# Sparse cross-attention's preparation joined into its main block, its last two tiles weighed by VectorE and its last sums in one group, and the alignment's two edge moves swapped

## The reference, cut to what matters

```python
R = D[i, j] + min(R[i-1, j], R[i, j-1], R[i-1, j-1])     # cost table, 64 x 1601 per batch
# then backtracking through R from the end gives which context rows belong to each row of x
```

```python
Q, K, V = split_heads(x @ Wq.T + bq), split_heads(ctx @ Wk.T + bk), split_heads(ctx @ Wv.T + bv)
scores = Q @ K.T / sqrt(8)
topk_scores, topk_indices = top_k(scores, 32)
context = softmax(topk_scores) @ V[topk_indices]
x = x + (merge_heads(context) @ Wo.T + bo)
```

## Time and profile before

| what | value |
|---|---|
| median of 3 executions | 4256.11 us (4254.29 to 4256.95) |
| the profiled execution: its time, its span | 4252.25 us, 4250.5 us |
| busy over the span: TensorE, VectorE, ScalarE, GpSimd | 82%, 77%, 65%, 34% |
| alignment's scans | about 139 to 312 us |
| sparse cross-attention with its preparation | about 2625 to 4038 us |

### The profile page before, as it was taken

One profiled execution on the slowest core, in us unless ns is written; L12 is line 12 of the kernel. 1 busy time (PEld: TensorE's weight loads), 2 busy tenths in 40 slices (PEclk: granted clock), 3 DMA queues, 4 the chain that ended last, 5 costly groups with the idle time before them and its releaser, 6 DMA issues. The chain is left out here.

```text
span 4250.5 us, 71372 instructions
## 1 busy us (share of the span) xinstructions
PE 3506.3 (82%) x25855; PEld 2847.3 (67%) x25855; DVE 3271.4 (77%) x5582; ACT 2742.5 (65%) x4270; POOL 1437.4 (34%) x1185
## 2 busy tenths in 40 slices
PE   6435748999999879999999986788888888888787
PEld 3334437999999657799999963466666666666676
DVE  4684877777777652787787755899999999999744
ACT  3112626666666443666666642799999999999832
POOL 0000502111111100211122010577777777777610
PEclk9555869999999889999999988899999999999998
DMA  8744001111111020111111000100000000100000
GB/s 275 117 47 124 4 28 45 40 40 32 32 35 30 14 77 14 47 32 32 40 34 38 17 16 10 38 18 30 16 17 32 16 17 16 32 16 9 1 24 19
DMA packets 186346, 161.34 MB, mean 38 GB/s; under 512 B 7996, under 2 KB 174092, under 8 KB 185996
## 3 DMA queue, kind: packets, MB, share of 16 engines
q1 hardware_dynamic: 182604, 142.83, 12.9%
q10 hardware_dynamic: 3392, 13.93, 0.9%
HBM read 127.36 MB, written 20.20 MB: 35 GB/s over the span
## 5 line engine op out<-in xcount | busy, mean ns | idle before, releaser
L559 PEld LDWEIGHTS psU<-ctxN,ST 128*128 128x128 f32 x6656 | 853.7, 191 | 98.4 <-issue 39.6
L559 PE MATMUL psU<-ctxN,ST 128*128 128x129 f32 x6656 | 868.1, 275 | 20.6 <-issue 20.6
L645 ACT ACTIVATE ST<-ST 128x512 f32<-128x512 f32 (+1 forms) x832 | 513.3, 625 | 167.0 <-DVE ST L747 163.1
L1188 DVE MAX8 top<-pairs 128x8 f32<-128x1602 f32 (+1 forms) x384 | 587.6, 1535 | 0.0
L1143 POOL TENSOR_TENSOR P<-P,EX 128x1601 f32<-128x1601 f32 x128 | 460.4, 3597 | 305.7 <-ACT P L1046 305.7
L747 DVE TENSOR_TENSOR ST<-ST,psB 128x512 f32<-128x512 f32 (+1 forms) x832 | 555.8, 677 | 3.4 <-PE psB L578 3.4
L733 DVE TENSOR_TENSOR psA<-psA,ST 128x512 f32<-128x512 f32 x640 | 446.2, 697 | 137.4 <-ACT ST L637 69.5
L947 PE MATMUL psU<-ctxN,PT 128*128 128x129 f32 (+1 forms) x3328 | 454.3, 291 | 3.3 <-ACT PT L1054 3.3
L947 PEld LDWEIGHTS psU<-ctxN,PT 128*128 128x128 f32 (+1 forms) x3328 | 427.0, 206 | 3.8 <-ACT PT L1054 3.8
L547 PE MATMUL psS<-statL,ctxH 128*128 128x512 f32 x832 | 393.3, 473 | 5.6 <-ACT ST L637 2.7
L925 PE MATMUL psS<-KT,stat 128*128 128x512 f32 (+1 forms) x1024 | 379.4, 513 | 17.4 <-DVE maxes L1166 16.4
(11 more groups left out here) (509 smaller groups left out, 6686.0 us busy)
## 6 DMA issues: line engine op xcount, KB each, us to landing
ctxN<-in_ctx SPq DMA_DIRECT2D x48, 768.0 KB
ahead_ctxT<-ctxT_scratch SPq DMA_DIRECT2D x32, 800.5 KB, 4.3
ctxT_scratch<-trn ACTq DMA_DIRECT2D x16, 800.5 KB
ctxT<-ctxT_scratch SPq DMA_DIRECT2D x16, 800.5 KB, 6.1
nat<-in_ctx SPq DMA_DIRECT2D x16, 768.0 KB
dist_scratch<-dd SPq DMA_DIRECT2D x8, 800.5 KB
skewed<-in_ctx SPq DMA_DIRECT2D x8, 768.0 KB
ctx_late<-in_ctx SPq DMA_DIRECT2D x8, 768.0 KB
```

Source lines behind the costliest of these rows:

```text
L559: last = pe.matmul(psU[:, q, 0:D + 1], ST[0:n, i % SLOTS, q * 128:q * 128 + 128], ctxN[0:n, j, k, 0:D + 1], start=(k == 0 and q % 2 == 0), ...
L645: act.activation(ST[0:n, i % SLOTS, :], ST[0:n, i % SLOTS, :], ACT.Exp).then_inc(exp_done, 1)
L1188: dve.max(top_t[:, 8 * n:8 * n + 8], own).then_inc(listed_early if n < 2 else listed_late, 1)
```

## The change

Four edits, all to the order and the place of work; what is computed stays the same.

1. The alignment: in TensorE's and in ScalarE's list the drift's edge is now moved ahead of the cost's in every iteration.
2. The preparation of the sparse cross-attention: the six small blocks are gone. The `layernorm` block now also loads the first batch's transposed context (one 800 KB transfer, fourth of nine) and fills the constants. All the rest stands in the lists of the large block: three transposes, the queries in two halves, the first keys and scores, and, between the first scores, the joined weights in four products (their copies are now ScalarE's), the bias row, and the addition of the bias to x (GpSimd, in iteration 2).
3. The last two tiles (126 and 127): ScalarE makes the mask in one step, and VectorE's one instruction `weigh` takes the minimum with the count and multiplies with the exponentials; in iteration 128 ScalarE exponentiates tile 127 and marks tile 126 before its other work.
4. The last output product is one group: 12 heads between the transposes and the values of tile 127, 4 heads at the end, one addition.

```diff
+        wide_Wo = P[:].rearrange("p j k -> p (j k)")[:, 0:H * D]
+        BY_VECTOR = T - 2
+        layernorm(c, [(W[:, 0, :], d["L3_xattn_Wq"]), (W[:, 1, :], d["L3_xattn_Wk"]),
+                      (W[:, 2, :], d["L3_xattn_Wo"]), (ctxT[:, 0, :], c.ctxT[0]), (WvN[:], d["L3_xattn_Wv"]),
+                      (bo[:], row_bcast(d["L3_xattn_bo"]))]
+                  + [(bias[:, n:n + 1], d[f"L3_xattn_{v}"].rearrange("(p a) -> p a", a=1))
+                     for n, v in enumerate(("bq", "bk", "bv"))],
+                  [(ctxN[:, j, :, D:D + 1], 1.0) for j in range(2)] + [(SS[:, j, K:KP], LOW) for j in range(3)])
...
-            @block.gpsimd
...
-                for j in range(2):
-                    pool.memset(ctxN[:, j, :, D:D + 1], 1.0).then_inc(filled, 1)
-                for j in range(3):
-                    pool.memset(SS[:, j, K:KP], LOW).then_inc(filled, 1)
-                pool.tensor_tensor(c.x[:], c.x[:], bc(c.bias_row[:].rearrange("p (a d) -> p a d", a=1), [128, NT, D]),
-                                   ALU.add).then_inc(filled, 1)
-                pool.wait_ge(filled, 6 + ONE)
...
+                def project_queries(n):
+                    pe.wait_ge(wt_ready, (3 if n else 1) + ONE)
+                    pe.matmul(psT[:, n, :], WT[:, 0, :], c.xnT[:, n * 512:n * 512 + 512], start=True, stop=True
+                              ).then_inc(qp_ready, 1)
+
+                def join_weights(n):
+                    if n < 2:
+                        pe.wait_ge(q_ready, n + 1 + ONE)
+                    else:
+                        pe.wait_ge(n_ready, n - 1 + ONE)
+                    pe.wait_ge(wo_spread, 4 * (n + 1) + ONE)
+                    pe.matmul(psT[:, n % 2, :], WvN[:], wide_Wo[:, n * 512:n * 512 + 512], start=True, stop=True
+                              ).then_inc(n_made, 1)
+
+                def join_bias():
+                    pe.wait_ge(cols_ready, 1 + ONE)
+                    pe.matmul(psU[:, 0:D], bias_cols[:], WoT, start=True, stop=True).then_inc(bias_made, 1)
+
+                def last_sums(heads):
+                    pe.wait_ge(ut_ready, T - 2 + ONE if heads[0] == 0 else T + ONE)
+                    if heads[0] == 0:
+                        pe.wait_ge(folded, T + ONE)
+                        pe.wait_ge(copied, T + ONE)
+                    for h in heads:
+                        last = pe.matmul(psS[:, 0:D], UT[:, (NT - 1) % 2, h, :, :], N[:, h, :], start=(h == 0),
+                                         stop=(h == H - 1))
+                    if heads[-1] == H - 1:
+                        last.then_inc(y_ready, 1)
...
+                for n in range(3):
+                    turn_weights(n)
+                project_queries(0)
+                pe.wait_ge(wt_ready, 2 + ONE)
                 for n in range(BLOCKS):
                     project(0, n)
                 scores(0)
+                project_queries(1)
+                join_weights(0)
                 scores(1)
+                for n in range(1, 4):
+                    join_weights(n)
+                join_bias()
...
+                        if t == T - 1:
+                            last_sums(range(H - 4))
                         values(t, 0)
...
-                for g in range(PARTS):
-                    sums(NT - 1, g, T)
+                last_sums(range(H - 4, H))
...
+                    if t >= BY_VECTOR:
+                        act.activation(P[:, j, :], sides[:], ACT.Relu, scale=-float(K), bias=rest[:, j:j + 1]
+                                       ).then_inc(marked, 1)
+                        return
...
+                    if s == 1:
+                        for n in range(1, 4):
+                            copy_joined(n)
...
+                    if s == T:
+                        exps(T - 1)
+                        mark(T - 2)
...
-                    if 0 <= s - 2 < T:
+                    if 0 <= s - 2 < T and s != T:
...
-                    if 0 <= s - 1 < T:
+                    if 0 <= s - 1 < T - 1:
...
+                    if t >= BY_VECTOR:
+                        pool.tensor_scalar(rest[:, j:j + 1], above[:, j:j + 1], -1.0, float(TOPK), ALU.mult, ALU.add
+                                           ).then_inc(rest_ready, 1)
...
+                    if s >= 2 and s - 2 < BY_VECTOR:
                         weigh(s - 2)
+                    if s == 2:
+                        pool.wait_ge(bias_ready, 1 + ONE)
+                        pool.tensor_tensor(c.x[:], c.x[:], bc(c.bias_row[:].rearrange("p (a d) -> p a d", a=1), [128, NT, D]),
+                                           ALU.add).then_inc(x_biased, 1)
...
+                    dve.wait_ge(marked, t + 1 + ONE)
+                    dve.wait_ge(spanned, 2 * t + 2 + ONE)
+                    dve.wait_ge(exp_done, t + 1 + ONE)
+                    dve.scalar_tensor_tensor(out=P[:, j, :], in0=P[:, j, :], scalar=span[:, j:j + 1], in1=EX[:, j, :],
+                                             op0=ALU.min, op1=ALU.mult).then_inc(weighed_late, 1)
...
+                for n in range(3):
+                    copy_turned(n)
+                dve.tensor_scalar(bias_cols[:], c.ones[:], bias[:, 2:3], None, ALU.mult).then_inc(cols_ready, 1)
+                scale_queries(0)
+                dve.wait_ge(wt_ready, 3 + ONE)
+                for h in range(H):
+                    dve.tensor_scalar(wide_Wo[:, h * D:h * D + D], WoT, c.headmask[:, h:h + 1], None, ALU.mult
+                                      ).then_inc(wo_spread, 1)
                 fold(0)
+                scale_queries(1)
...
+                    if s == 1:
+                        dve.wait_ge(bias_made, 1 + ONE)
+                        dve.tensor_tensor(c.bias_row[:], psU[:, 0:D], bo[:], ALU.add).then_inc(bias_ready, 1)
+                    if BY_VECTOR <= s - 2 < T:
+                        weigh(s - 2)
...
-                for g in range(PARTS):
-                    add(NT - 1, g)
-                dve.wait_ge(y_added, PARTS * NT + ONE)
+                add(NT - 1, 0)
+                dve.wait_ge(y_added, PARTS * (NT - 1) + 1 + ONE)
...
-            layernorm(c, [(W[:, 0, :], d["L3_xattn_Wq"]), (W[:, 1, :], d["L3_xattn_Wk"]),
...
-            turn_all(c, [(WT[:, n, :], W[:, n, :]) for n in range(3)])
-            head_blocks(c, s2, WvN[:], WT[:, 2, :], N)
-
-            spread_bias(c, bias[:, 2:3], WT[:, 2, :], bo)
-            project(c, QT, WT[:, 0, :], c.xnT, bias[:, 0:1], 8.0 ** -0.5)
-        topk_cross_attention(c, N, QT, WT[:, 1, :], bias[:, 1:2])
+    topk_cross_attention(c)
...
                     for s in range(STEPS + LAG):
+                        if s - LAG >= 1:
+                            move_drift(s - LAG)
                         if s < STEPS:
                             if s == RING:
                                 pe.wait_ge(row_carried, 1 + ONE)
                             move_cost(s)
-                        if s - LAG >= 1:
-                            move_drift(s - LAG)
...
                     for s in range(STEPS + LAG):
+                        if s >= LAG:
+                            set_drift_edge(s - LAG)
                         if s < STEPS:
                             if s == RING:
                                 carry_row()
                             set_edge(s)
-                        if s >= LAG:
-                            set_drift_edge(s - LAG)
```

More of the change, by code:

```diff
@@ L827, in topk_cross_attention @@
         UT = c.sb(st, "UT", [128, 2, H, 2, S])
+        N = c.sb(st, "N3", [128, H, D])
+        QT = c.sb(st, "QT", [128, B * S])
+        W = c.sb(st, "W", [128, 3, D])
+        WT = c.sb(st, "WT", [128, 3, D])
+        WvN = c.sb(st, "WvN", [128, D])
+        bo = c.sb(st, "bo", [128, D])
+        bias = c.sb(st, "biases", [128, 3])
+        bias_cols = c.sb(st, "bias_cols", [128, 128])
+        WkT, WoT, bk = WT[:, 1, :], WT[:, 2, :], bias[:, 1:2]
+        flat_N = N[:].rearrange("p h d -> p (h d)")
+        wide_Wo = P[:].rearrange("p j k -> p (j k)")[:, 0:H * D]
[6 more added lines that the diff above has]
+                  [(ctxN[:, j, :, D:D + 1], 1.0) for j in range(2)] + [(SS[:, j, K:KP], LOW) for j in range(3)])
         psS = c.ps(st, "psS", [128, 2048])
@@ L857, in topk_cross_attention @@
         y_ready, y_added = c.sem("y_ready"), c.sem("y_added")
-        with nc.Block() as block:
-            @block.gpsimd
-            def _(pool):
-                for j in range(2):
-                    pool.memset(ctxN[:, j, :, D:D + 1], 1.0).then_inc(filled, 1)
-                for j in range(3):
-                    pool.memset(SS[:, j, K:KP], LOW).then_inc(filled, 1)
-                pool.tensor_tensor(c.x[:], c.x[:], bc(c.bias_row[:].rearrange("p (a d) -> p a d", a=1), [128, NT, D]),
-                                   ALU.add).then_inc(filled, 1)
-                pool.wait_ge(filled, 6 + ONE)
         with nc.Block() as block:
@@ L929, in turn @@
                 def turn(t, q):
-                    if q == 0:
```

(29 more changed lines are left out.)

50 lines of the change are left out of this document (26 added, 24 removed).

## The result

| | kernel before | changed kernel |
|---|---|---|
| median | 4256.53 us (4 runs, 4254.29 to 4264.06) | 4221.16 us (4 runs, 4217.97 to 4224.12) |
| ratio, 95% interval | | 0.9919, 0.9906 to 0.9932 |
| profiled execution, span | 4252.25, 4250.5 us | 4224.12, 4222.4 us |

The kernel is faster by 35.4 us, and 44.8 were forecast. The time is 9.9 us above the forecast and 0.2 outside its range. Cut at the start of each stage's layernorm (ScalarE's table load, L205), and in the sparse cross-attention at fold(0) and fold(127), the two profiled executions differ by

What follows compares the result with a forecast made beforehand. VectorE and ScalarE were taken to share the loop's bound, TensorE and GpSimd having slack. Alignment 15.3, preparation 25.3, bias addition -1.6 and tail 5.8 sum to 44.8 us, so 4256.11 - 44.8 = 4211.3 us, range 4203 to 4221.

Steps and rivals of the forecast that it cites:

- What bounds the kernel: Sparse cross-attention loop: VectorE and ScalarE share the bound, busy 196.5 and 194.7 of 200 us; TensorE (164.8) has slack.
- Alignment 15.3: Alignment: drift's edge first saves 0.74 us in 15 iterations without a comparison, 0.09 in 47 with one; 15.3 us.
- Rivals 1 and 2: Alignment: cost's edge late, iteration 2.07, total 4218.0 us, chance 0.12; swap does nothing, 4226.6 us, chance 0.04.
- Preparation 25.3: Sparse cross-attention's preparation: first transpose to fold(0) takes 12.0 us instead of 38.15, block ahead 0.8 late; gain 25.3.
- the first transposes near 2616.8: Preparation, profile after: first transposes start near 2616.8, everything being 15.3 us earlier, with fold(0) 12.0 later.
- Rival 3: Preparation: GpSimd's `stat` held up by VectorE's sixteen spreads, scores 1.5 us late, total 4212.8 us; chance 0.12.
- Bias addition, 1.6: Loop, iteration 2: GpSimd's 2.34 us addition delays ScalarE's `mark(1)` some 1.9, about 0.3 lost, the rest stays; cost 1.6.
- Rival 4: Loop: ScalarE's delay at the start returns at each of 15 later batches, 28.5 us more, 4239.8 us; chance 0.04.
- Tail 5.8: Last two tiles and sums: 6.8 - 1.6 - 3.5 + 4.8 = 6.5 us, taken as 5.8, ends 3.5 and 7.
- Rival 5: Unchanged loop becomes dearer, as by tiles' new memory places; 0.35 us a tile takes back all 44.8; chance 0.02.
- Sum: Whole kernel: 15.3 + 25.3 - 1.6 + 5.8 = 44.8 us gain, subtracted from the median 4256.11 for 4211.3 us.
- 4206 to 4220: Whole kernel: the forecast's own range by the ends of its terms was put above 4206 to 4220 us.

Runs made afterwards that it cites:

- the two steadied loops: Three extra unread TensorE products in tiles with a key block: kernel before 4257.22 us, ratio 0.9985; changed kernel 4212.99 us, ratio 0.9893.
- The delays: A write of zeros (1024 or 2048 columns) on VectorE behind fold(0): changed kernel 4221.77 and 4223.20 us; kernel before 4263.19 and 4262.73 us.
- no_tail: The changed kernel with the old tail (GpSimd weighs the last two tiles, ScalarE's old order, last sums in four groups): 4224.62 us, ratio 0.9909.

## Why the prediction was wrong

- **What bounds the kernel.** The loop as VectorE's and ScalarE's was right for the tiles without a long wait. But the earlier trace rows has PEclk at 0.97, and I read TensorE's slack of a sixth as cover enough. It is not where the clock falls ahead of the values.
- **Alignment 15.3.** Right: 2.27 and 1.62 in the rows, 16.1 as the mean over 18 stages. Rivals 1 and 2 are out, no iteration of 2.07 is there.
- **Preparation 25.3.** Right in sum, 25.8 (24.0 with keys at the lower clock). Its pieces were off both ways: the first transpose came 2.22 us behind the last `xnT` (2621.82) where it was 1.07 before, so the block ends 1.15 late, for 0.8; the keys took 3.10, for 4.0, or 4.75 in the other profile. Its sign "the first transposes near 2616.8" didn't come: they start at 2624.04, since the alignment gave 14.55 instead of 15.3, the block ended 1.15 late, and the untouched stages between lost 6.1. The ends are added wrongly too: 0.4 with keys of 3.9 gives 25.8 and not 26.2, 2.0 with keys of 4.8 gives 23.3.
- **Rival 3, `stat` held by the spreads.** Out, and the other way round: `stat` took 1.90, and VectorE was held. The line of the spreads (ns min/median/max) has one of 1958 ns among fifteen of 274:

```profile
L1345 DVE TENSOR_SCALAR P<-WT,headmask x16: 271/274/1958, 2627.7 to 2632.3; 128x128 f32<-128x128 f32 x16
```

  The Trainium skill's SBUF — State Buffer, section Who interferes with whom, has an exclusive lock between these two engines. The row agrees: GpSimd's `stat` begins at 2627.83 and ends at 2629.73, the second spread begins 0.02 us behind it and is done only 0.08 behind its end. It lay beside keys and scores and cost nothing.
- **Bias addition, 1.6.** The start is right, the wait of 1.70 for `rest` is there. The way on is not: "about 0.3 being lost; from there it stays" gave 1.6, but by fold(12) the loop was 3.0 to 4.7 us late, and by fold(21) most of that was made good. That the two steadied loops differ by 1.0 at the end, near the 1.6, is in part luck. Rival 4, its return at 15 batches, is out.
- **Tail 5.8.** Right: 6.16; `weigh` took 1.89 for 1.8.
- **Rival 5 and "Sum".** Here the prediction failed. "The durations are those of the profiled execution" and "4256.11 - 44.8" take all that isn't changed as fixed. In the profiled pair the loop lost 9.1 us and the untouched stages 9.3, together 18.4, of which 1 to 1.6 are the change's. I gave "something in the unchanged loop becomes dearer" a chance of 0.02, by the tiles' places in memory. It did become dearer, by another mechanism: TensorE's lower clock fell ahead of the values of more tiles, and VectorE waited. Most of this is no property of the changed program: with the key blocks' waits filled the two loops differ by 1.0 us, and the old loop took up to 1331.1 us in other profiles. For the untouched stages no experiment was made; over all eighteen profiles the three stages named above take 110.0 to 113.2, 81.1 to 83.7 and 149.4 to 156.0 us, old and new preparation alike, so the profile of before was low in them and that of after high in the first. The median of three that I subtracted from, 4256.11, is 5.2 us below the median of 72 (4261.3). From that, 44.8 leads to 4216.5; the eight runs of the changed kernel have 4221.2.
- **The range.** "4206 to 4220" is not what its ends add up to: 16.7 + 26.2 - 0.3 + 7 = 49.6 and 8.6 + 23.4 - 2.3 + 3.5 = 33.2 give 4206.5 to 4222.9, and the measured 4221.16 lies inside that. It would have been luck: the range held terms for each edit and none for this scatter. The runs of the kernel before alone reach from 9 us below their median to 17 above.

**What stays open.** Against the median of 72 the gain is 40.1 us, and the terms at their places add up to 46 (16.1 + 25 - 1.0 + 6.1). The 6 us between are two differences of means: the loops, 3.9 us where 1.0 is the program's by the steadied pair, and the stages that the change doesn't touch, together 2410.1 us in six kernels with the old preparation (2408.5 to 2412.6) and 2412.9 in twelve with the new one (2407.5 to 2417.8). Both are of the size of their scatter, and I can't say that they are chance. Nor did I find out what decides behind which waits the clock falls. The delays don't tell, since in `no_tail` the tiles moved as far without one.

## What to carry to other kernels

Terms read where the work is done were good to 1.3 us here, but for the delay that enters a full loop; the whole was off by 10, because the rest of the program doesn't stand still: before a sum is made against a profile, look whether that execution is a typical one, and give the scatter of the untouched part its own term. Where TensorE has slack but waits 2 us in a tile, look at the granted clock behind the wait and at who waits for the next products. Filling such waits can pay (8 us here) although TensorE isn't the bound, if the filling ends before the wait would, and needs no wait that holds TensorE up. And one profile of each kernel can't show an effect of 3 us on a loop that scatters by 5; where the added work sits, the times from fold to fold could.

## What the hardware showed that was not expected

- TensorE's granted clock falls to 1.2 GHz inside a loop where it is busy 83% of the time, mostly behind single waits of 1.6 to 3.2 us, and not behind each of them; 16 products then take up to 3.6 us instead of 1.96.
- The old loop, its instructions unchanged, takes from 1322.0 to 1331.1 us in five profiles, with 8 to 12 long waits, and part of these stand at other tiles in a second profile of the very same kernel.
- An instruction of VectorE of 0.27 us took 1.96 beside one of GpSimd of 1.90.
